# Four-network GNN kernel: the node update of the third network and its norms as one skewed block with nodes on partitions, and the first transposing reads issued beside a product

## The reference, cut to what matters

```python
def _L2_gnn_ref(nodes, edge_index, edge_attr, ...):
    messages = concatenate([nodes[senders], edge_attr], -1) @ W_message.T
    aggregated = segment_sum(messages, receivers)
    node_input = concatenate([nodes, aggregated], -1)
    h = layer_norm(relu(node_input @ W1.T + b1), ln1_g, ln1_b)
    node_out = layer_norm(relu(h @ W2.T + b2), ln2_g, ln2_b)
    return layer_norm(nodes @ W_node.T + node_out, ln_g, ln_b)
...
x = x + _L2_gnn_ref(h, ...)
h = maximum(_layernorm(x), 0.0)
x = x + _L3_gnn_ref(h, ...)      # first step of it: h @ W1, scaled by 1/sqrt(degree)
```

## Time and profile before

| | us |
|---|---|
| median of 3 runs (lowest, highest) | 3652.15 (3646.51, 3656.03) |
| the profiled execution | 3643.69 |
| its span, first to last instruction | 3641.9 |
| TensorE busy | 3231.3 (89%) |
| VectorE busy | 902.0 (25%) |
| ScalarE busy | 730.5 (20%) |
| GpSimd busy | 151.6 (4%) |
| mean granted clock of TensorE | 0.952 of 2.4 GHz |

### The profile page before, as it was taken

The page is one execution under the profiler, slowest core; times in us unless marked ns, Lnnn a source line. Parts: engine busy times, 40 slices in busy tenths (PEclk is TensorE's granted clock), DMA queues, the critical chain, the costliest instruction groups (busy, mean ns, idle before and its releaser), DMA issues. The chain is left out here.

```text
span 3641.9 us, 46107 instructions
## 1 busy us (share of the span) xinstructions
PE 3231.3 (89%) x18047; PEld 1759.9 (48%) x18047; DVE 902.0 (25%) x1294; ACT 730.5 (20%) x1066; POOL 151.6 (4%) x115
## 2 busy tenths in 40 slices
PE   1899599976998799999989989979998779996997
PEld 1788455543443355555555555534553215554554
DVE  6999522223002500100010010041002361003002
ACT  4899411122002300100010010010003430002002
POOL 4000033310000000000000000000000000000000
PEclk9999799987999899999999999989999789998998
DMA  6234899925762265455455545516550005552553
GB/s 232 72 125 136 226 159 163 177 38 135 153 144 46 89 182 145 136 152 148 119 169 147 144 147 145 146 40 171 152 136 1 0 36 144 144 145 76 141 145 106
DMA packets 740967, 465.50 MB, mean 128 GB/s; under 512 B 349231, under 2 KB 735956, under 8 KB 739702
## 3 DMA queue, kind: packets, MB, share of 16 engines
q1 hardware_dynamic: 706456, 425.29, 46.3%
q10 hardware_dynamic: 32702, 31.44, 2.8%
q0 software_dynamic: 1664, 6.92, 0.6%
HBM read 316.13 MB, written 67.19 MB: 105 GB/s over the span
## 5 line engine op out<-in xcount | busy, mean ns | idle before, releaser
L1257 PE MATMUL acc<-tbuf,hs 128*128 128x448 fp8e4 x9604 | 1831.6, 353 | 18.5 <-DVEq L1291 18.3
L1257 PEld LDWEIGHTS acc<-tbuf,hs 128*128 128x128 f16 x9604 | 938.1, 98 | 917.4 <-issue 58.6
L1309 DVE SCALAR_TENSOR_TENSOR B<-acc,scales,C 128x448 f32 x84 | 57.3, 682 | 1551.2 <-PE acc L1257 1551.2
L1526 PE MATMUL acc<-tbuf,hs 128*128 128x512 fp8e4 (+1 forms) x1300 | 284.8, 373 | 24.4 <-DMA tbuf<-table 24.4
L668 ACT ACTIVATE stage<-quad 128x784 fp8e4<-128x784 f32 x392 | 291.5, 828 | 7.2 <-PE quad L688 5.7
L688 PE MATMUL quad<-K,S 128*128 128x196 bf16 x1568 | 277.7, 250 | 15.0 <-DVE K L628 7.2
L692 PE MATMUL deg<-K,S 128*128 128x196 bf16 x1568 | 276.5, 247 | 0.0
L1408 PE MATMUL acc<-tbuf,hs 128*128 128x512 fp8e4 (+1 forms) x1300 | 266.7, 369 | 0.4 <-issue 0.4
L1283 ACT ACTIVATE H<-B,vectors x56 | 37.4, 668 | 1062.1 <-DVE B L1314 1062.1
L1526 PEld LDWEIGHTS acc<-tbuf,hs 128*128 128x128 f16 x1300 | 121.0, 99 | 151.5 <-issue 32.0
L1408 PEld LDWEIGHTS acc<-tbuf,hs 128*128 128x128 f16 x1300 | 123.5, 98 | 143.7 <-issue 3.3
(11 more groups left out here) (242 smaller groups left out, 1658.7 us busy)
## 6 DMA issues: line engine op xcount, KB each, us to landing
tbuf<-table SPq DMA_DIRECT2D x343, 448.0 KB, 3.5
tbuf<-table SPq DMA_DIRECT2D x343, 336.0 KB, 3.1
table<-stage SPq DMA_DIRECT2D x6, 5488.0 KB, 19.5
h_kept<-H SPq DMA_DIRECT2D x4, 3136.0 KB, 14.9
feat<-in_edge_attr_dram ACTq DMA_DIRECT2D x27, 448.0 KB, 5.5
C<-factors ACTq DMA_DIRECT2D x2, 3136.0 KB, 12.3
table<-stage SPq DMA_DIRECT2D x2, 2744.0 KB, 12.1
A<-x_kept ACTq DMA_DIRECT2D x1, 3136.0 KB, 10.6
```

Of the source, the lines that this page charges most:

```text
L1257: mm = nc.tensor.matmul(acc[h][:, 0:HALF], k.hs[:, kb, part, :], counts[:, (r - lo) * STRIP + h * HALF:(r - lo) * STRIP + (h + 1) * HALF], ...
L1309: ins = V.scalar_tensor_tensor(dst[:, at], acc[h][:, 0:HALF], scale, k.C[:, at], ALU.mult, ALU.mult)
L1526: mm = T.matmul(acc[g % 2][:, 0:n * P], k.hs[:, j, part, :], counts[:, :, j // 2, :, j % 2], start=(j == 0 and part == 0), stop=(j == NL - ...
```

## The change

Four things are changed; sizes and results stay the same.

1. The blocks from `load_ea(wait=True)` to the `split_rows` of the fourth network's first layer are replaced by one block, `update_nodes`. It goes by 13 groups of 4 blocks of 128 nodes (the last group has one block) with nodes on partitions: the matmuls use blocks of H, B and C as the stationary operand and the weights as the moving one. Mean and variance come from `bn_stats` and `bn_aggr` on VectorE, a norm is applied by ScalarE with a scale and a bias per partition, one block of 128 at a time (L2081). It runs 19 iterations; in iteration `it` each step works on its own group (`it` minus a lag of 0 to 6). Each step's result has one PSUM bank.
2. The message weights are multiplied into W1 beforehand (`cross`, `cross_e`, two products in `prepare`); the row of biases b1 comes in as a row of ones, which GpSimd writes to C in `load_ea`.
3. The first 8 transposing reads are issued in the block of the first `product` instead of in `split_rows`.
4. In the last stage A is added when VectorE takes the turned strip out of PSUM, and ScalarE no longer copies.

`table_buffer` is smaller for `pool_neighbours`, semaphores are reused, and `layer_norm` loses its `times` part. The core of the diff:

```diff
-        for l in range(2):
+        def dense(l, first_buffer=None):
+
             v0 = 6 * l
...
+        overflow(k, k.spill_rows, k.spill_dst, k.spill_src, D, H, B, True, ready=True)
+        with table_buffer(k) as tbuf:
+            dense(0, tbuf)
+            split_rows(k, H, False, 1, None, None, tbuf, False)
+            pool_sources(k, B, tbuf, 1)
+        overflow(k, k.spill_rows, k.spill_dst, k.spill_src, D, H, B, True)
+        dense(1)
...
         overflow(k, k.spill_rows, k.spill_src, k.spill_dst, D, H, B)
-        load_ea(k, C, wait=True)
-        product(k, [(W["msg"], B), (W["msg_e"], C[0:3 * DE])], B, ACT.Identity, k.zero[:, 0:1])
-        product(k, [(W["up_h"], H), (W["up_m"], B)], C, ACT.Relu, vec(16))
-        layer_norm(k, C, B, C, vec(17), vec(18))
-        product(k, [(W["down"], B)], C, ACT.Relu, vec(19))
-        layer_norm(k, C, B, C, vec(20), vec(21))
-        product(k, [(W["node"], H), (k.idf[:, :], B)], C, ACT.Identity, k.zero[:, 0:1])
-        layer_norm(k, C, H, C, vec(22), vec(23))
-        with nc.sbuf_tensor("times", [WCH, NW, CH], F32) as times:
-            layer_norm(k, A, H, B, add=True, times=times)
         for l in range(2):
             weight = W[f"g{l}"]
-            split_and_pool(k, H, True, 6 + l, B, 2, weight=weight, own=weight, load_factor=False)
+            if l:
+                split_and_pool(k, H, 6 + l, B, 2, weight=weight, own=weight, load_factor=False)
+            else:
+                with table_buffer(k, True) as tbuf:
+                    update_nodes(k, B, w, weight, 6, tbuf)
+                    pool_neighbours(k, B, 2, weight, tbuf, False, H, None, 6)
...
 def product(k, terms, dst, func, bias, stats=False, tbuf=None):
+        if tbuf is not None:
+            @block.sync
+            def _(sp):
+                for h in range(2):
+                    load_turned(k, sp, tbuf, h, h)
...
 def load_ea(k, into):
+        @block.gpsimd
+        def _(pool):
+            nc.gpsimd.memset(into[3 * DE:3 * DE + 1, :], 1.0)
...
 def elu_stage(k, sums, bias, dst, out=None):
+    def leave(V, dve, s):
+        dve.wait_ge(o_T.h, o_T.at(s + 1))
+        for i, (b0, b1) in enumerate(((0, 4), (4, US))):
+            at = slice((s * US + b0) * P, (s * US + b1) * P)
+            V.tensor_tensor(sums[:, at], k.bank[2 * (s % 2) + i][:, 0:(b1 - b0) * P], k.A[:, at], ALU.add
+                            ).then_inc(o_copied.h, 1)
...
-                    pe.wait_ge(done.h, done.at(s + 1))
+                    pe.wait_ge(top.h, top.at(s + 1))
```

More of the change, by code:

```diff
@@ L849, in small_loads @@
     loads += [(k.W[name], a, w_in) for name, a in straight]
+    loads.append((k.weights[3 * DE:3 * DE + 1, n, :], w["L2_gnn_b1"].rearrange("(a f) -> a f", a=1), w_in))
     k.w_in = 16 * len(loads)
@@ L856, with layer_norm @@
 WCH = NCH // NW
-def layer_norm(k, src, dst, squares, gain=None, shift=None, add=False, times=None):
+def layer_norm(k, src, dst, squares, gain=None, shift=None, add=False):
     nc = k.nc
@@ L999, in layer_norm, with product @@
               ln_spread=NCH, ln_final=NCH, ln_added=NCH if add else 0)
-def product(k, terms, dst, func, bias, stats=False):
+def product(k, terms, dst, func, bias, stats=False, tbuf=None):
     nc = k.nc
@@ L1121, in turned_done, with split_and_pool @@
             k.sem(f"table_in{h * 4 + b}").base += 16 * len([g for g in range(h, NSG, 2) if b < width(g)])
-def split_and_pool(k, v, over_src, at, dst, factor, weight=None, own=None, load_factor=True, layer=None, extra=None):
-    with table_buffer(k) as tbuf:
-        split_rows(k, v, over_src, at, weight, own, tbuf, layer is not None)
-        if over_src:
-            pool_neighbours(k, dst, factor, own, tbuf, load_factor, v, layer, at)
-        else:
-            pool_sources(k, dst, tbuf, at)
+def split_and_pool(k, v, at, dst, factor, weight=None, own=None, load_factor=True, layer=None):
+    with table_buffer(k, True) as tbuf:
+        split_rows(k, v, True, at, weight, own, tbuf, layer is not None)
+        pool_neighbours(k, dst, factor, own, tbuf, load_factor, v, layer, at)
 def split_rows(k, v, over_src, at, weight, own, tbuf, keep):
@@ L1873, in _ @@
                         V.tensor_tensor(dst[:, at], dst[:, at], k.C[:, at], ALU.mult)
-                    else:
-                        V.tensor_tensor(dst[:, at], dst[:, at], k.A[:, at], ALU.add).then_inc(done.h, 1)
+                if out is not None and s >= 2:
+                    leave(V, dve, s - 2)
+            if out is not None:
+                leave(V, dve, NU - 1)
         @block.scalar
@@ L1920, in _, with load_ea @@
                 sp.wait_ge(o_out.h, o_out.at(16 * (NU + 1)))
-    k.advance(elu_low=NU, elu_top=NU, elu_exp=NU, elu_done=0 if out is None else NU)
-def load_ea(k, into, wait=False):
+    k.advance(elu_low=NU, elu_top=NU, elu_exp=NU)
+def load_ea(k, into):
     nc = k.nc
```

353 lines of the change are left out of this document (303 added, 50 removed).

## The result

| | before | after |
|---|---|---|
| runs, us (median) | 3646.51 to 3656.03 (3652.2) | 3573.84, 3568.66, 3559.42, 3566.29 (3567.5) |
| profiled execution, us (span) | 3643.69 (3641.9) | 3573.84 (3572.1) |
| mean granted clock | 0.952 | 0.948 |

The changed kernel is faster: ratio 0.9768, 95% interval 0.9744 to 0.9792, or 84.7 us between the medians. The forecast was 3572, in the range 3535 to 3612.

A forecast was written before the change was run, and what follows sets the result against it. The prediction took a VectorE-ScalarE loop, 14.1 us per group, to bound the new block. Terms -79 + 5 - 4.7 + 0.4 = -78 took the profiled 3643.69 to 3565.7, median 3572, range 3535 to 3612.

The forecast's parts named there:

- The ring: Update block: VectorE and ScalarE wait on each other in a loop closing once per iteration, 14.1 us per full group.
- some ten hand-offs at 0.05: Update block: passing work between engines adds 0.05 us each per iteration, 9.0 us over 18 turns.
- The sum: Update stretch: block 199 us, 3.35 before it and some 1.2 behind, so 203 for 282.5, or -79.
- rival 1: Update block: TensorE at half clock becomes the limit, 18 us per group instead of 14.1; 3619 us, chance 0.12.
- Rival 2: Update block: 128x128 norms at 0.30 us save 18, free hand-offs save 9; 3545 us, chance 0.13.
- Rival 3: Update block: ScalarE waits for TensorE's product of the same iteration, engines take turns; block 356, total 3725 us, chance 0.03.
- `load_ea`: Block in which GpSimd writes 6272 ones on one partition while all engines wait at its end: +5 us.
- Reads: First network: eight transposing reads moved beside the first product, -17.1 us in `split_rows`, +12.4 in the product's block: -4.7.
- Last stage: Last stage's strips: VectorE's add split in two from PSUM at 1.37 us, period 3.1 for 2.8: +0.4 us.
- Table reload: Update block: ScalarE reloads its function table at each root, 46 us; 3618 us, chance 1 in 100.
- The offset: Whole kernel: median stands 8.5 us above the profiled execution before, a little less after; 3565.7 becomes 3572.
- The inner range: Whole kernel: the forecast's own range from the ends of `load_ea` and reads and +-15 us on 199, 3552 to 3595.

## Why the prediction came out

- *What bounds the block:* right. The ring, and VectorE's wait for the third norm, stand as drawn; the wide instruction on and off it shows it. But the prediction also said "I am wrong if ScalarE's or VectorE's waits in a full iteration are ended by TensorE", and such waits are there, 2.07 and 1.06 us. That sign was badly chosen: a wait counts only if it is on the ring, and the doubled products show that these aren't.
- *Its size:* 14.1 forecast, 13.47 measured. Norms 6.30 and 6.29, statistics 3.2 and 3.23, wide pair 1.50 and 1.55. The term that was most off is "some ten hand-offs at 0.05". The ring passes from one engine to another only twice outside the root, with 0.04 and 0.03 us between end and start (2855.14 + 0.18 to 2855.36, 2858.45 + 3.17 to 2861.65), and the prices from runs cover them; the gap of the earlier trace rows is one between two instructions of VectorE. Aggregates were 1.08, not 1.2, the low part 0.64, not 0.75. Over the 18 turns of the ring the hand-offs were 9.0 us of the sum, aggregates and low parts a bit over 1 us each.
- *The sum:* block, its neighbours and the first product 203 forecast, 196.5 measured; -79 became -86. Two errors partly cancelled: from the first statistics to the end 182.0 us for 192.1 (the terms just named), and ahead of them 14.4 (2751.58 to 2766.01) for 3.35 + 8.1. The five loads landed 5.9 us into the block, where I took 3.1 from the landing of one read the earlier trace rows.
- *TensorE:* clock 0.75 over the block, between the ends named; the doubled products show that rival 1 was no danger here. The Trainium skill (TensorE: Matmul & The Clock Gate, "HAM oscillation — how this bites in real kernels") has TensorE at half rate where waits part its bursts. The trace agrees: the clock is 1.00 during the wait of 4.13 us, falls to 0.50 after the products resume and is near 1.00 again for the next group's products, so that an iteration has 0.75 or 0.87; behind waits of at most 1.3 us it stays at 1.00, and in the skewless order a stretch has 0.55 to 0.66. TensorE's work of an iteration was 7.98 us at clock 1.00 (window of the order without the wait), where 6.9 were forecast. It never set the period in the changed kernel, but was part of the ring in the experiment that put two norms of ScalarE behind Z.
- *Rival 2 (shorter ring):* its reason in part (hand-offs free), but not norms at 0.30: 0.393 each.
- *Rival 3:* its mechanism is real: where ScalarE's norms stood behind a product of the same iteration, full iterations were 12.7 to 13.8 us for 10.2. One group at a time, engines wholly in turn, costs more than the 356 I priced, 415.5 us, since that price has TensorE's products in the chain but not the four rounds of norm. The lags keep it away.
- *`load_ea`:* +5 forecast, +4.85 measured. *Reads:* -4.7 forecast, -7 measured in repeats: the product block came to 27.7, not 29.0, and `split_rows`' gain was 18, not 17.1. *Last stage:* +0.4 forecast, -1.5 measured; 1.37 for a price that was 1.16 here is 1.5 of it in 7 strips. *Table reload:* none, the changed kernel's profile has the same three loads.
- *The offset:* I carried 6.3 of the 8.5 us between the profiled execution and the median. It was right to, for a reason that I didn't know: one stage of the profile of before was 12.7 us quick. Parts measured (-88.9, with the reads at -7 rather -89.7), less some 4 us that stay open, give -85.7, near the medians' -84.7, whose interval is some 76 to 93.
- *Luck:* that 3572 stands 4.5 us from the median is in part luck. The parts came to 11 us more than the -78 summed; the open 4 us of the untouched stage and the 2 us that I took off the offset made up over half of that. The inner range, 3552 to 3595, doesn't come out of its terms: added plainly their ends are 31 below and 26 above, 3541 to 3598. The range given at last covers these.

## What to carry to other kernels

When engines take steps in program order, draw the loop that closes through each engine once per iteration, price it from instruction runs (here without anything added for hand-offs), and test it with one added instruction on it and one off it. Before moving work off that loop, list for each in-order engine what stands behind every wait for another engine's step of the same iteration; such a wait with a needed step behind it ate all of an expected gain of 36 to 42 us here, and reordering the steps around it took 42.9 us off that block. Two profiles of one kernel differed by 12.7 us in one stage with 49 transposing reads; before explaining a difference in an untouched stage, profile the old kernel again.

## What the runs showed of the hardware that was not expected

- Issuing four transposing reads took SyncE 13.4 to 14.1 us, eight 26.6 to 28.8, beside a product as beside `split_rows`; the block's end waits for the issuing, so four fit behind a product of 16.5 us and eight don't.
- More work made TensorE quicker per product: with 147 products added the granted clock rose from 0.75 to 0.83, and each cost 0.14 us busy, where one takes 0.217 at clock 1.00.
- The end of the stage with 49 transposing reads varied by 12.7 us between two executions of the same kernel (778.14 and 790.80), and the whole spans by 12.9 (3641.9 and 3654.8). Of the stretches compared, that from the first product to `pool_sources` differed by 1.2 us (85.2 and 86.4), the update stretch by 0.2 (282.5 and 282.3).
